# Masks of two second attention passes as a minimum on VectorE, a bias on GpSimd, and another slice order

## The reference

```python
for l in range(2):
    h = shift_token(x); q, k, v = split(h @ wqkv)       # 8 heads of 64
    q, k = rotary_xpos(l2norm(q) * qs, l2norm(k) * ks)
    x = x + local_attention(q, k, v) @ wo               # window: i - 64 <= j <= i, within a band
    h = layer_norm(shift_token(x)) * lg + lb
    a, g = split(h @ w1 + b1)
    x = x + (a * gelu(g)) @ w2 + b2
```

## Time and profile before

| | |
|---|---|
| median of 3 runs | 2754.06 us (2751.47 to 2760.95) |
| the profiled execution | 2756.0 us |
| its span, first to last instruction | 2754.2 us |
| TensorE busy | 2051.2 us, 74% |
| weight loads | 1166.5 us, 42% |
| ScalarE busy | 1416.9 us, 51% |
| VectorE busy | 1352.0 us, 49% |
| GpSimd busy | 532.1 us, 19% |
| mean granted TensorE clock | 0.849 of full speed |

### The profile page before, as it was taken

One profiled execution on the slowest core, in us unless ns is written; L12 is line 12 of the kernel. 1 busy time (PEld: TensorE's weight loads), 2 busy tenths in 40 slices (PEclk: granted clock), 3 DMA queues, 4 the chain that ended last, 5 costly groups with the idle time before them and its releaser, 6 DMA issues.

```text
span 2754.2 us, 51642 instructions
## 1 busy us (share of the span) xinstructions
PE 2051.2 (74%) x20756; PEld 1166.5 (42%) x20756; DVE 1352.0 (49%) x3140; ACT 1416.9 (51%) x3619; POOL 532.1 (19%) x601
## 2 busy tenths in 40 slices
PE   1405574779787978798878887898789787978767
PEld 0303223444453445344634463445444453445434
DVE  2512333554546463746474646555654546463442
ACT  0311361387537662776367735764477537762433
POOL 0270200312022110402040304020302022110220
PEclk9957776789888988898889897998889888988787
DMA  5362300200020001100020002000200020000000
GB/s 187 102 173 64 77 2 12 48 2 2 13 52 1 2 7 34 24 3 5 14 47 3 1 14 51 3 1 13 51 2 2 13 52 1 2 7 12 1 0 5
DMA packets 97224, 75.91 MB, mean 28 GB/s; under 512 B 44451, under 2 KB 87804, under 8 KB 94814
## 3 DMA queue, kind: packets, MB, share of 16 engines
q1 hardware_dynamic: 92894, 66.35, 9.7%
q0 software_dynamic: 4096, 6.32, 1.5%
HBM read 41.55 MB, written 33.16 MB: 27 GB/s over the span
## 4 chain that ended last, share of the span: by engine, by line
PE 45%; ACT 16%; DVE 14%; issue 8%; POOL 5%; DMA 1%; SPq 0%; POOLq 0%; DVEq 0%; ACTq 0%
PE PS L945 5%; PE PS L1581 4%; ACT work_a L1146 4%; PE PS L1616 4%; ACT work_b L1812 3%; PE PS L1718 3%; POOL work_b L2021 3%; DVE work_a L1265 3%; PE PS L1689 3%; PE PS L1731 2%; DVE work_a L1309 2%; PE PS L921 2%; PE PS L1651 2%; ACT work_a L1163 2%; PE PS L1680 2%
## 5 line engine op out<-in xcount | busy, mean ns | idle before, releaser
L1146 ACT ACTIVATE work_a<-PS,work_a 128x512 bf16<-128x512 f32 (+3 forms) x512 | 263.4, 530 | 79.3 <-DVE work_a L1265 77.8
L2021 POOL TENSOR_TENSOR work_b<-work_b,tables 128x256 f32<-128x256 f32 x256 | 212.0, 848 | 450.7 <-DVE work_b L1908 450.7
L1812 ACT ACTIVATE work_b<-PS,neg_max 128x192 f32<-128x192 f32 (+1 forms) x512 | 201.9, 417 | 121.1 <-DVE neg_max L1948 75.0
L1265 DVE TENSOR_REDUCE work_a<-PS 128x2 f32<-128x1024 f32 (+3 forms) x256 | 200.8, 821 | 106.5 <-PE PS L897 103.6
L1163 ACT ACTIVATE work_a<-PS 128x1024 f32<-128x1024 f32 (+1 forms) x192 | 169.6, 883 | 121.2 <-PE PS L927 119.1
L1581 PE MATMUL PS<-wqkv,hT 128*128 128x512 f32 x384 | 200.6, 654 | 7.5 <-DVE work_b L1908 6.2
L1616 PE MATMUL PS<-k,q 64*128 64x192 f32 (+1 forms) x1024 | 162.3, 454 | 58.7 <-ACT shiftT L1798 27.9
L2035 POOL TENSOR_TENSOR rstd_b<-var_eps_b,minus_half 128x4 f32<-128x4 f32 x16 | 16.4, 1027 | 876.1 <-DVE var_eps_b L121 876.1
L945 PE MATMUL PS<-work_a 128*64 128x512 f32 (+3 forms) x1024 | 179.8, 454 | 0.0
L1616 PEld LDWEIGHTS PS<-k,q 64*128 64x128 f32 x1024 | 109.7, 266 | 112.2 <-ACT work_b L1812 39.8
L1828 ACT ACTIVATE work_b<-PS 128x768 f32<-128x768 f32 (+1 forms) x128 | 97.2, 759 | 97.6 <-PE PS L1659 97.6
(11 more groups left out here) (295 smaller groups left out, 4218.4 us busy)
## 6 DMA issues: line engine op xcount, KB each, us to landing
work_a<-stack_d SPq DMA_DIRECT2D x32, 512.0 KB, 9.6
stack_d<-parts SPq DMA_DIRECT2D x48, 192.0 KB, 3.5
stack_d<-parts SPq DMA_DIRECT2D x32, 128.0 KB, 2.7
x_all<-in_L_attn_x_dram SPq DMA_DIRECT2D x4, 512.0 KB
...
```

Of the source, the lines that this page charges most:

```text
L1146: nc.scalar.activation(dump0[:, n % 2 * T:n % 2 * T + (i + 1) * P], PS[:, a:a + (i + 1) * P], ACT.Exp, bias=neg_max0[:, k:k + 1], accum_ou ...
L1265: nc.vector.reduce_max(neg_max0[:, 2 * g * NT + i:(2 * g + 2) * NT:NT], at[:, :, Q_AT[i]:Q_AT[i] + (i + 1) * P], AX_X, negate=True).then_i ...
L1812: nc.scalar.activation(dump2[:, n % 4 * 256:n % 4 * 256 + w], PS[:, a:a + w], ACT.Exp, bias=neg_max2[:, k:k + 1], accum_out=sums2[:, k:k + ...
L2021: nc.gpsimd.tensor_tensor(to[:, n, :, r, :], src[:, n, :, 1 - r, :], table(2 * n + 1, t)[:, 32 * r:32 * r + 32].unsqueeze(1).to_broadcast( ...
```

## The change

**Masks.** The mask matmuls of both second passes go. The tiles `limitT16` and `band_limitT16` hold 3e38 where a score stays and -1e30 where it is masked. After the scores of a unit VectorE takes the minimum of scores and limit, in place in PSUM, and ScalarE waits for that (`cutT`). In A the two blocks of a unit's second kind are laid so that both diagonal blocks are neighbours (`K_AT`), and only the diagonal blocks are covered: 128, 256 and 128 columns of each of two heads. In B all columns are covered, 384 or 320 of each of two heads. **Bias.** The bias matmuls go; the bias is loaded to all 128 partitions, and GpSimd adds it to y after its power, VectorE's last addition waits for it (`biased`). **Order.** Another `A_AHEAD`.

```diff
-    c[:, C_CAUSALT:C_CAUSALT + P] = np.where(p > f, NEG, 0.0)
+    c[:, C_CAUSALT:C_CAUSALT + P] = np.where(p > f, NEG, BIG)
...
-    c[:, C_BANDT:C_BANDT + P + WIN] = np.where((gap < 0) | (gap > WIN), NEG, 0.0)
+    c[:, C_BANDT:C_BANDT + P + WIN] = np.where((gap < 0) | (gap > WIN), NEG, BIG)
...
-        K_AT = {0: 0, 1: 0, 3: 384, 2: 0}
+        K_AT = {0: 0, 1: P, 3: 0, 2: 0}
...
-                    n = len(KTILES[u])
-                    for e in range(2):
-                        to = bank(e).rearrange("p (n c) -> p n c", c=P)[:, 0:3 * n - 2:3, :]
-                        last = nc.tensor.matmul(to, ident16[:, :], causalT16[:, :].unsqueeze(1).to_broadcast([P, n, P]),
-                                                start=False, stop=True, skip_group_check=True)
                     last.then_inc(sa["scoresT"], 1)
...
-                    act.wait_ge(sa["scoresT"], ofa("scoresT", m + 1))
+                    act.wait_ge(sa["cutT"], ofa("cutT", m + 1))
...
                 if m == 0:
                     dve.wait_ge(sa["max"], ofa("max", maxes_done(UNITS - 1)))
                     shifts(1)
+                if m < UNITS:
+                    dve.wait_ge(sa["scoresT"], ofa("scoresT", m + 1))
+                    n = len(KTILES[m % 3]) * P
+                    scores = PS[:, 0:1024].rearrange("p (e c) -> p e c", e=2)[:, :, 0:n]
+                    nc.vector.tensor_tensor(scores, scores, limitT16[:, 0:n].unsqueeze(1).to_broadcast([P, 2, n]),
+                                            ALU.min).then_inc(sa["cutT"], 1)
...
-                    for e in range(2):
-                        if x:
-                            rows = bandT16[:, :]
-                        else:
-                            rows = bandT16[:, 0:KX].unsqueeze(1).to_broadcast([P, 2, KX])
-                        last = nc.tensor.matmul(bank(4 + e, 0, W2K[x]), ident16[:, :], rows, start=False, stop=True,
-                                                skip_group_check=True)
...
-                    if c == 0:
-                        nc.tensor.matmul(o, ones_row, b2_sb[:, l * P:(l + 1) * P], start=(t == 0),
-                                         stop=(t == 0), skip_group_check=True)
...
-                    act.wait_ge(s["scoresT"], past("scoresT", m + 1))
+                    act.wait_ge(s["cutT"], past("cutT", m + 1))
...
+                if m < 8:
+                    dve.wait_ge(s["scoresT"], past("scoresT", m + 1))
+                    scores = PS[:, 4 * BANK:6 * BANK].rearrange("p (e c) -> p e c", e=2)[:, :, 0:W2K[m % 2]]
+                    if m % 2:
+                        limit = band_limitT16[:, :].unsqueeze(1).to_broadcast([P, 2, 320])
+                    else:
+                        scores = scores.rearrange("p e (n c) -> p e n c", c=KX)
+                        limit = band_limitT16[:, 0:KX].unsqueeze(1).unsqueeze(1).to_broadcast([P, 2, 2, KX])
+                    nc.vector.tensor_tensor(scores, scores, limit, ALU.min).then_inc(s["cutT"], 1)
...
             dve.wait_ge(s["w2_mm"], past("w2_mm", 1))
+            dve.wait_ge(s["biased"], past("biased", 1))
             nc.vector.tensor_tensor(y[:, :], y[:, :], bank(6), ALU.add).then_inc(s["y_out"], 1)
...
             nc.gpsimd.tensor_tensor(rstd_b[:, :], var_eps_b[:, :], minus_half[:, 0:NT], ALU.pow).then_inc(s["rstd"], 1)
+            gp.wait_ge(s["low"], past("low", 1))
+            gp.wait_ge(s["step_mm"], past("step_mm", 1))
+            nc.gpsimd.tensor_tensor(y[:, :].rearrange("p (t f) -> p t f", f=P),
+                                    y[:, :].rearrange("p (t f) -> p t f", f=P),
+                                    b2_sb[:, l * P:(l + 1) * P].unsqueeze(1).to_broadcast([P, NT, P]), ALU.add
+                                    ).then_inc(s["biased"], 1)
...
-        A_AHEAD = (17, 0, 2, 1, 0, 0, 0, 0, 0, 4, 2, 0, 2, 0, 1, 0, 0, 0, 2, 2, 2, 1, 2, 1, 2, 1, 2, 2, 1, 6, 3, 0, 1, 1,
+        A_AHEAD = (17, 0, 3, 1, 0, 0, 0, 0, 1, 2, 2, 2, 0, 1, 1, 0, 2, 0, 2, 2, 2, 2, 1, 1, 2, 1, 1, 1, 3, 3, 3, 0, 0, 1,
```

47 lines of the change are left out of this document (25 added, 22 removed).

## The result

| | before | after |
|---|---|---|
| median of 4 runs | 2756.37 us (2751.47 to 2760.95) | 3001.51 us (2982.31 to 3011.68) |
| ratio | 1 | 1.0881, 95% interval 1.0819 to 1.0944 |
| span of the profiled execution | 2754.2 us | 2993.9 us |
| mean granted TensorE clock | 0.849 | 0.818 |
| time at the lower clock level | 835 us | 1094 us |

The account below looks back on a forecast made before the run. TensorE was taken to bound one stage, VectorE or a three-engine loop others. Steady batches +13 us, seven times +91, with the ends +110 on 2754.06: 2864 us; whole range 2700 to 2930.

Parts of the forecast that it names:

- the sum of the steady batch: Each batch beside its neighbour: stage +12, layer 1 +5, layer 0 -4, so +13 us, seven times +91.
- VectorE's total: VectorE's busy time over the kernel: 211 us of minima added, from 1352 to some 1563 us.
- each price of the minimum: VectorE's minimum in the second passes: 0.415 and 0.69 us in A, 0.956 and 0.82 us in B.
- both lone loops: Second passes running alone: A's head pair from 5.00 to 5.7 us, two units of B from 4.50 to 5.65.
- The rival that TensorE stays the wall: Removed matmuls come out whole where the passes are paired: 2665 us, chance 0.22.
- Layer 1 ... +5: Layer 1 per batch: 2.7 first minimum, 3.6 units, 1.3 triangle masks, 3 solve round trips, -4 first pass, -1.65 bias: +5 us.
- Layer 0 ... -4: Layer 0's first-pass stretches and second pass: minima hide behind ScalarE, more A units fill the shifts' gap: -4 us a batch.
- first pass "-4": Layer 1's first pass: the two triangle products leave it, -4 us a batch.
- The ends: Kernel start with A alone +7.7 us, last batch with B alone +15.0 less 3.3 for bias: together +19 us.
- What goes ... 48 + 52 us: Mask matmuls of both second passes hold 48 us (A) and 52 us (B) of the path.
- GpSimd's addition ... at nothing: Bias addition after the layer norm's power, 1267 ns, 20 us before it is needed: costed at nothing.
- The clock's case: TensorE falls to 1.2 GHz in the lone second-pass loops: +115, 2980 us, half of it 2920; chance 0.12.

Follow-up runs that it names:

- the ceiling of 40 us: Bias on GpSimd, old order, no second-pass masks at all, against the kernel before: ratio 0.9706, 2674 us; against the run with only the bias moved, 40 us.
- the new order alone: The kernel before with the new slice order and nothing else, masks and bias still on TensorE: 2861.41 us, ratio 1.0395.
- the bias alone: The kernel before with the bias of the second product added by GpSimd and nothing else: 2710.25 us, ratio 0.9851.
- the run with A's masks alone: The kernel before with the minimum on VectorE in stream A's second pass only, old order: 2946.11 us, ratio 1.0710.
- the run with matmuls in layer 1's waits: The changed kernel plus 12 unread matmuls in layer 1, eight ahead of the normed rows' transposes, four behind: ratio 1.0727 to the kernel before.

## Why the prediction was right in its sign and wrong in its size

The step that failed is the sum of the steady batch: +13 us was forecast, +32.1 measured (288.6 to 320.7), and most of the difference lies in the terms of layer 1 (+5) and layer 0 (-4).

**Right.** VectorE's total, each price of the minimum, both lone loops, the start of the kernel, and the mechanism: a minimum is late where VectorE has a long piece ahead of it. The stage from layer 0's output projection to layer 1's first scores was forecast at +12 and came to 95.3 - 80.6 = +14.7. Within it: +5.1 to the transposes of the normed rows (6.3 forecast, though the wait in it was 5.4 and not 4.4), -1.4 to those of y (-1.5), and from there to the first scores 56.6 against 45.5 us, +11.1 (7.2): the six units ahead of the projections take 12 us, the projections then nothing more. The rival that TensorE stays the wall fails by the ceiling of 40 us.

**"Layer 1 ... +5"** was +13.3. Its parts: the second pass +5.9 where 2.7 + 3.6 + 1.3 + 3 = 10.6 were forecast, bias -1.8 (-1.65). What failed is the solve's round trips, priced at 3 us and put into the second pass: with the solves spread, the delta rule's products land behind that pass, between the transposes and the second product, +10 us a batch, an entry that the sum did not have at all. It stands in the new order alone too (17.4 us), so it is the table's. 5.5 of the 10 us are the clock (18.8 against 13.3 us with TensorE kept busy), the rest the product itself, which no longer lies in the norm's shadow.

**"Layer 0 ... -4"** was +3.9, and first pass "-4" was +1.4. The credit for more units of A near the second half of the shifts was taken from the order on TensorE; on ScalarE the same units stand ahead of B's copy of the shifts. Both come with the table alone (100.5 and 40.0). Together: (13.3 - 5) + (3.9 + 4) + (14.7 - 12) = 18.9 us a batch, seven times 132 us, where the seven batches were short by 226.7 - 91 = 136. The ends were 6.5 us too high. The last batch came to +5.4 where 15.0 - 3.3 = 11.7 were forecast: its two second passes grew by 5.2 and 5.4 us in place of 7.5 each, and the rest of it shrank by some 5 us in place of 3.3. These sizes hold the clock too: against the bias alone, whose passes ran at 1.00, the same passes are 15.7 us longer.

**"What goes ... 48 + 52 us"** was 40 us in all. The path price of a mask was read in the lone passes and used for all. In A's lone pass it is right (from the first scores to the last, 36.05 us without masks and 41.64 with: 0.70 us a head pair for the 0.75 forecast). Elsewhere the price was not met, in the last batch because the clock fell (21.0 us without masks, 20.7 with). That most masks of the woven part lie beside a wait that ends elsewhere is likely and not shown; there too the clock took some, in layer 1's second pass, 24.0 us at 0.91 for 23.1 at 0.99. This did little harm to the sum, which was made by stages, but a larger gain than exists stood behind the first rival.

**"GpSimd's addition ... at nothing"** was right on its own queue and wrong beside it: it starts with the norm multiplies, the first of which waits it out, so that the four take 2.06 us for 1.12. That is the extra microsecond of the wait behind the norm.

**The clock's case** was given 0.12 and 2920 to 2980 us. Its mechanism is shown (42 us at one place; 16 at another, in the run with A's masks alone), its place was wrong in part: I put it into the loops of the second passes, and the 42 us were in a stretch where TensorE has no gap. In the changed kernel's lone passes it can be little, they ran at or under the forecast (5.67 and 5.58 us); in layer 1's projections and woven second pass its share is open. The Trainium skill (TensorE: Matmul & The Clock Gate, What's actually happening) has the throttled state as the default that activity releases; by that, added matmuls should shorten a stretch, and the run with matmuls in layer 1's waits agrees, 13.3 us for 18.8.

The Trainium skill (Perfetto Trace Analysis, Identifying the Most-Contended Engine) would have the engine with the highest occupancy optimized first, but warns against matmul busy time and judges TensorE by its share of peak and its weight loads. The weight loads are 42% of the span in the kernel before, under ScalarE's 51%, so its rule does not name TensorE as plainly as the prediction had it, and the runs agree with the warning: of 124 us taken from the engine with 74% of matmul time 40 reach the time.
